# First cross attention of a four-layer kernel: a changed order of key projections, key parts and value casts

## The reference, cut to what matters

```python
x = x + _L0_xattn_ref(_layernorm(x), ctx, Wq, bq, Wkv, bkv, Wp, bp)

def _fq_sym(x, axis):            # fake quantisation to 127 steps
    s = max(max(abs(x), axis) / 127.0, 1e-08)
    return clip(round(x / s), -127, 127) * s

q = (x @ Wq + bq).reshape(1, 256, 16, 16)
kv = (cond @ Wkv + bkv).reshape(1, 4096, 2, 16, 16)
k, v = kv[:, :, 0], kv[:, :, 1]
q = _fq_sym(q * scale, axis=-1)  # one scale for a query and head
k = _fq_sym(k, axis=-1)          # one scale for a key and head
v = _fq_sym(v, axis=keys)        # one scale for a column, over all 4096 keys
attn = _fq_unsigned(softmax(q @ k.T), axis=-1)
return (attn @ v) @ Wp + bp
```

## Time and profile before

| | us |
|---|---|
| median of 3 runs | 1547.86 (1547.01 to 1548.96) |
| profiled execution, its own time | 1544.69 |
| its span, first to last instruction | 1542.9 |
| first stage in it, up to the last update of x | 0 to 332.4 |
| the loop over key pairs in it | about 8 to 142 |

### The profile page before, as it was taken

One profiled execution on the slowest core, in us unless ns is written; L12 is line 12 of the kernel. 1 busy time (PEld: TensorE's weight loads), 2 busy tenths in 40 slices (PEclk: granted clock), 3 DMA queues, 4 the chain that ended last, 5 costly groups with the idle time before them and its releaser, 6 DMA issues. The chain is left out here.

```text
span 1542.9 us, 23951 instructions
## 1 busy us (share of the span) xinstructions
PE 1380.5 (89%) x7964; PEld 978.2 (63%) x7964; DVE 1090.4 (71%) x2242; ACT 858.8 (56%) x2296; POOL 576.3 (37%) x643
## 2 busy tenths in 40 slices
PE   7867999966998789988789999999998989999979
PEld 5643444445866357767557778788877446666667
DVE  4688999925774665754568776675654779999963
ACT  2446999932124282435444645554554589999931
POOL 2236777730000002520536523532400047777710
PEclk9986999967999899997989999999999999999989
DMA  4000454554341404000200000000002343333110
GB/s 150 1 1 21 93 96 97 95 161 158 139 171 34 102 28 105 29 1 1 82 15 0 15 14 1 15 1 1 1 1 84 114 144 123 123 95 112 42 61 9
DMA packets 125073, 97.88 MB, mean 63 GB/s; under 512 B 84499, under 2 KB 100883, under 8 KB 124310
## 3 DMA queue, kind: packets, MB, share of 16 engines
q1 hardware_dynamic: 124950, 96.35, 21.6%
HBM read 79.28 MB, written 0.26 MB: 52 GB/s over the span
## 5 line engine op out<-in xcount | busy, mean ns | idle before, releaser
L601 ACT ACTIVATE x_v_full<-banks,x_neg_max,x_q_scale 128x1024 uint8<-128x1024 f32 x128 | 152.6, 1197 | 6.1 <-DMA x_v_full<-x_v_full 2.8
L708 DVE TENSOR_REDUCE x_row_max<-banks 128x1 f32<-128x512 f32 x248 | 151.6, 681 | 4.8 <-PE banks L381 4.8
L213 PE MATMUL banks<-a_w_ring,x_normed_T 128*128 128x512 f32 x320 | 146.4, 598 | 4.9 <-DVE a_r L3256 4.9
L538 POOL CAST x_v_full<-x_v_full 128x1024 f16<-128x1024 uint8 x128 | 131.5, 1044 | 50.4 <-DMA x_v_full<-x_v_full 46.2
L2735 DVE TENSOR_TENSOR ctx_tokens<-ctx_tokens,banks 128x512 f32<-128x512 f32 x128 | 87.8, 686 | 82.2 <-ACT x_weights_T L2621 60.3
L2453 PE MATMUL banks<-ctx_tokens,x_kT 128*128 128x512 f32 x272 | 140.0, 602 | 2.8 <-ACT ctx_tokens L2615 2.2
L2474 PEld LDWEIGHTS banks<-x_v,x_weights_T 128*128 128x128 f32 x896 | 113.0, 194 | 20.8 <-issue 17.5
L2474 PE MATMUL banks<-x_v,x_weights_T 128*128 128x129 f32 x896 | 118.1, 278 | 2.1 <-ACT x_weights_T L2631 2.1
L2569 POOL TENSOR_TENSOR ctx_tokens<-ctx_tokens 128x512 f32<-128x512 f32 (+1 forms) x48 | 65.9, 1373 | 141.4 <-DVE ctx_tokens L2715 141.4
L381 PE MATMUL banks<-x_kT_parts,x_qT_int 64*128 64x512 bf16 x512 | 109.8, 408 | 6.9 <-DVE x_row_max L708 4.1
L3146 POOL TENSOR_TENSOR a_rms<-a_rms,a_minus_half 128x4 f32<-128x4 f32 x64 | 64.9, 1014 | 115.7 <-ACT a_rms L3076 115.7
(11 more groups left out here) (533 smaller groups left out, 3278.6 us busy)
## 6 DMA issues: line engine op xcount, KB each, us to landing
a_w_ring<-in_L_attn_WB_T SPq DMA_DIRECT2D x16, 512.0 KB, 3.7
a_w_ring<-in_L_attn_WC_T SPq DMA_DIRECT2D x16, 512.0 KB, 5.5
f_w_gate_up<-in_L_ffn_gate_up SPq DMA_DIRECT2D x9, 736.0 KB, 4.3
f_w_down<-in_L_ffn_down SPq DMA_DIRECT2D x9, 512.0 KB, 5.2
ctx_tokens<-in_ctx SPq DMA_DIRECT2D x16, 256.0 KB, 6.2
x_wq<-in_L_xattn_Wq_T SPq DMA_DIRECT2D x8, 512.0 KB, 3.7
a_w_ring<-in_L_attn_Wth_T SPq DMA_DIRECT2D x8, 512.0 KB, 3.8
a_bias_ring<-in_L_attn_B_bias_perm SPq DMA_DIRECT2D x16, 256.0 KB, 4.9
```

The lines of the kernel that those rows point to most:

```text
L213: last = nc.tensor.matmul(out, lhsT, rhs, start=(i == 0), stop=(i == len(pairs) - 1))
L538: nc.gpsimd.tensor_copy(pf[:, q % WIDE], pt8[:, q % TURNED]).then_inc(s.unpacked, 1)
L601: nc.scalar.activation(eb[:, q % RING], k.ps[:, 2 + 2 * (q % 2):4 + 2 * (q % 2), :].rearrange("p a n -> p (a n)"), ACT.Exp, bias=nb[:, v % ...
L708: nc.vector.reduce_max(mx[:, u % 2, i:i + 1], k.bank(MBANK[m % 3]), AX.X).then_inc(s.max_taken, 1)
```

## The change

In the first stage:

- TensorE projects key pair j+1 in step j, ahead of the transposes of pair j-3 (in step 3 the query transposes come first). Pair 0 is projected in step 0 as before.
- ScalarE makes the middle part of pair j-1 ahead of the first part of pair j. The copy of the value scales (step 11) moves to the front of its step. In the last step with a key, 15, the copies of transposed pair 12 move ahead of the first part.
- The four casts of the values go from GpSimd (steps 13 to 16) to ScalarE (steps 12 to 15), in front of the first part.
- After its loop ScalarE evaluates one exponential of one element.
- VectorE combines the four maxima of the values two at a time in steps 4, 6 and 8, not in one reduction in step 8.

In `l0_ffn` the semaphore `first_pair` is replaced by the existing `w_loaded[11]`.

```diff
@@ TensorE
-                    if j < NP:
-                        project_keys(j)
+                    if j == 0:
+                        project_keys(0)
                     if j == 1:
                         project_queries()
                     if j == 3:
                         transpose_queries()
+                    if j + 1 < NP:
+                        project_keys(j + 1)
                     if j >= 3:
                         transpose_keys(j - 3)
@@ GpSimd
-                    if NP // 2 + 5 <= j < NP // 2 + 9:
-                        g = j - NP // 2 - 5
-                        pool.wait_ge(s.v_int_ready, g + 1)
-                        nc.gpsimd.tensor_copy(vq[:, VG * g:VG * (g + 1)], vi[:, g]).then_inc(s.v_ready, 1)
@@ ScalarE
+                    if j == NP // 2 + 3:
+                        act.wait_ge(s.vscale_in_psum, 1)
+                        nc.scalar.copy(vscale[:].rearrange("p r n -> p (r n)"), k.bank(7)).then_inc(s.vscale_ready, 1)
+                    if 1 <= j < NP + 1:
+                        m = j - 1
+                        act.wait_ge(s.rest_ready, m + 1)
+                        nc.scalar.copy(part(m, 1), kr[:, m % 2]).then_inc(s.mid_ready, 1)
+                    if j == NP - 1:
+                        take_keys(j - 3)
+                    if NP // 2 + 4 <= j < NP // 2 + 8:
+                        g = j - NP // 2 - 4
+                        act.wait_ge(s.v_int_ready, g + 1)
+                        nc.scalar.copy(vq[:, VG * g:VG * (g + 1)], vi[:, g]).then_inc(s.v_ready, 1)
                     if j < NP:
                         act.wait_ge(s.kf_ready, j + 1)
                         if j >= 3:
                             act.wait_ge(s.kT_in_psum, 2 * (j - 2))
                         nc.scalar.copy(part(j, 0), kf[:, j % 3]).then_inc(s.hi_ready, 1)
-                    if 1 <= j < NP + 1:
-                        m = j - 1
-                        act.wait_ge(s.rest_ready, m + 1)
-                        nc.scalar.copy(part(m, 1), kr[:, m % 2]).then_inc(s.mid_ready, 1)
...
-                    if j >= 3:
+                    if j >= 3 and j != NP - 1:
                         take_keys(j - 3)
-                    if j == NP // 2 + 3:
-                        act.wait_ge(s.vscale_in_psum, 1)
-                        nc.scalar.copy(vscale[:].rearrange("p r n -> p (r n)"), k.bank(7)).then_inc(s.vscale_ready, 1)
+                act.wait_ge(s.filled, 1)
+                nc.scalar.activation(warm[:], k.ones[0:1, 0:1], ACT.Exp)
@@ VectorE
                         link(nc.vector.tensor_reduce(vm[:, g], vf[:, VG * g:VG * (g + 1)].rearrange("p t d -> p d t"), AX.X, ALU.max, apply_absolute_value=True))
+                        if g == 1:
+                            link(nc.vector.tensor_tensor(vmax, vm[:, 0], vm[:, 1], ALU.max))
+                        if g == 2:
+                            link(nc.vector.tensor_tensor(vmax, vmax, vm[:, 2], ALU.max))
                     if j == NP // 2:
-                        nc.vector.tensor_reduce(vmax, vm[:].rearrange("p g d -> p d g"), AX.X, ALU.max).then_inc(s.vmax_ready, 1)
+                        nc.vector.tensor_tensor(vmax, vmax, vm[:, 3], ALU.max).then_inc(s.vmax_ready, 1)
```

More of the change, by code:

```diff
@@ L261, in l0_xattn @@
         attn = sb("attn", [P, B, D])
+        warm = sb("first_exp", [1, 1])
         vdiag = attn[:].rearrange("p r (c t) -> p r c t", c=DC)
@@ L844, in l0_ffn @@
         code = sb("fp4_code", [P, MLP_HALF], U16)
-        first_pair = ctx.enter_context(nc.semaphore("f0_first_pair"))
         def load(sp):
             sp.dma_start(wg[:], A["L0_ffn_gate_w_T"].rearrange("(c p) n -> p c n", p=P)).then_inc(k.w_loaded[2], 16)
-            sp.dma_start(wgu[:, 0], A["L0_ffn_gate_up"][0]).then_inc(first_pair, 16)
-            sp.dma_start(wd[:, 0], A["L0_ffn_down"][0]).then_inc(first_pair, 16)
+            sp.dma_start(wgu[:, 0], A["L0_ffn_gate_up"][0]).then_inc(k.w_loaded[11], 16)
+            sp.dma_start(wd[:, 0], A["L0_ffn_down"][0]).then_inc(k.w_loaded[11], 16)
         layernorm(k, load)
@@ L882, in gate_up @@
                     if n == 0:
-                        pe.wait_ge(first_pair, 32)
+                        pe.wait_ge(k.w_loaded[11], 32)
                     else:
```

## The result

| | before | after |
|---|---|---|
| median, its range, runs | 1547.43 (1546.38 to 1548.96), 4 | 1532.72 (1529.65 to 1536.07), 4 |
| profiled execution, its own time | 1544.69 | 1536.07 |
| its span | 1542.9 | 1534.3 |

The ratio is 0.9906, interval [0.989, 0.9922]: faster by 14.7 us, where 15.5 were forecast. The two profiled executions are only 8.6 us apart. That of before lies 1.7 us under the fastest of the four runs in the table, that of after is the slowest of its four, so the sizes of the steps are better read between marks inside the stage. The first key reaches VectorE at 17.52 us before and at 18.52 after, a difference that lies ahead of the change; I count from there.

The account below looks back on a forecast made before the run. Hand-overs between engines bound the second stretch, VectorE's row maxima (97% busy) the main loop. 4.0 + 1.4 + 1.1 + 1.5 + 5.7 - 1.9 + 2.0 + 1.1 + 0.6 = 15.5 us, giving 1532.4 us; range 1527.5 to 1539.5.

Parts of the forecast that it names:

- Query hole +4.0: First stretch: TensorE's 3.99 us idle time before the query transposes goes, as key pair 2 is projected earlier; gain 4.0 us.
- clock +1.4: Two sets of 16 query transposes, slowed by TensorE's lower clock level after the idle time, run faster; gain 1.4 us.
- one projection ahead +1.1: TensorE projects pair 8 in front of the transposes of pair 4, which no longer delay it; gain 1.1 us.
- rival 2: TensorE's idle time before the query transposes stays, the margin being 0.4 us; 5.4 us less gain, 1537.8 us; chance 0.08.
- +1.5: VectorE's 1.89 us reduction over the values becomes a two-input maximum of 0.42 us; gain 1.5 us.
- +5.7: Second stretch: VectorE's waits shrink, 2.7 us for projections and 3.0 for the value scales; gain 5.7 us.
- Interference +2.0: VectorE's scale instructions and key products are slowed less once value casts leave GpSimd; gain 2.0 us, 2.5 still allowed.
- late last cast -1.9: Last step with a key: ScalarE's value cast, priced at 1.8 us, no longer hides behind VectorE; loss 1.9 us.
- Rival 1: VectorE and GpSimd get in each other's way in every step; 6.7 us less gain, 1539.1 us; chance 0.13.
- Tail +1.1: Last first part to the first head's last row maximum: two ScalarE copies move ahead, GpSimd's subtraction partly shows; gain 1.1 us.
- Table +0.6: Exponential table load, 1.28 us before the first exponential, moves beside the preceding work; VectorE's 0.60 us wait goes; gain 0.6 us.
- Rival 4: Main loop: TensorE stays at its lower clock; 24 slow quarter heads cost 15.5 us, all 128 end near 1614; chance 0.03.

Follow-up runs that it names:

- again: Unchanged kernels run once more for a second profile: the changed kernel 1532.72 us (ratio 0.9904), the kernel before 1547.79 us (ratio 0.9999).
- the pairs: Changed kernel with one DMA transpose for two quarters (64 in place of 128): 1520.2 us, ratio 0.9817; the same edit in the kernel before: 1534.63 us.

## Why the prediction was right

Counted from the first key, with the two "again" profiles where they bear on it:

- **Query hole +4.0, clock +1.4, one projection ahead +1.1.** The query transposes come 4.16 us earlier, key 8 6.4 earlier (62.04 to 55.61), where 6.5 were forecast. The margin of 0.4 us held, so rival 2 is out; the kernel without TensorE's order shows the hole at its old 3.99.
- **Up to the last key**, the terms named so far with +1.5, +5.7 and +2.0 make 15.7; measured 15.6. The reduction of the values was shown by itself at 1.5, TensorE's order by itself at 9.0 for its forecast 9.2 (4.0, 1.4, 1.1 and 2.7). That 15.7 met 15.6 is in part luck. VectorE's scale instructions and key products, over keys 8 to 15 and above their undisturbed 0.18 and 0.69 us, lose 4.7 us before and 3.5 after: interference gave 1.2 where 2.0 were forecast. The waits gave the difference back: what is left of the second stretch's 9.15 us behind that 1.2 and the 1.5 of the reduction is 6.5, for a forecast of 5.7. And of the 5.7 the split between the two orders did not hold: TensorE's alone takes 2.5 from the second stretch, the rest without it 8.9, where 6.5 were forecast (1.5, 2.0 and 3.0).
- **Interference +2.0** and **late last cast -1.9**: putting the casts back shows the move itself at 2.1 and 1.9. The +2.0 was a net figure, though, and the net is the 1.2 above: of the 4.7 us 3.5 are left, where 2.5 had been allowed, since a fuller VectorE meets GpSimd oftener (with the casts on GpSimd it is 5.6). The cast took 1.90 us, where a straight line through two shorter copies gave 1.8. Rival 1 (every step hit) fell, though GpSimd's subtraction was hit in half of them: four of the last eight took 2.0 to 2.5 us, each beside a value product. The next product of a key was hit only now and then (1.58 at 48.13 us). The Trainium skill (GPSIMD Engine Reference, Key points) names VectorE instructions with two SBUF inputs as those that contend with GpSimd. By that rule the trace agrees: the value product reads two SBUF tiles, and the subtraction beside it went from 1.16 to 2.49 us. The prediction drew from the rule that the last key product would be hit; it took 2.30 us before, beside a cast on GpSimd, and 0.69 after, when GpSimd was idle (116.44 us).
- **Tail +1.1**: mis-sized, 0.5. The last key to the last maximum took 1.4 us longer (10.21 to 11.59), where 0.8 was forecast from +1.1 and -1.9; with the casts on GpSimd it took 9.72, 0.5 less than before. The kernel with the middle part behind has nearly the same tail (11.42). The likely reason, as the rows have it: the subtraction of the last pair itself (1.15 us at 120.12) still has to pass before the middle part can start, and with the late cast the two copies were no longer what it stood behind. That last clause is a reading of the time line and was not tried by itself.
- **Table +0.6**: 0.3 to 0.4. From the last maximum to the first exponential 2.53 us became 0.82; 1.28 of these 1.7 are the load, and the other 0.4 comes from no edit that was taken out singly (the gap is 0.82 or 1.25 in variants with the early load, 2.10 or 2.53 in kernels without it). From the last maximum to quarter 20 the gain is 0.35 us (29.74 to 29.38), and without the one-element exponential it goes. The prediction was right to discount a gain in front of a busy loop, but named the wrong engine for it: where the head start is lost, ScalarE waits for TensorE at its lower clock. Rival 4 had said that with a denser start nothing is lost; the denser start lost the head start of 1.4 us.
- **"In the main loop VectorE sets the pace"**, and at the head of the prediction "VectorE is 97% busy [...] so that stretch moves as a block". The block did move as one, from quarter 20 to quarter 60 within about 0.1 us, so the sum took no harm; the reading was wrong all the same. SyncE's issues set the length of the loop, as the pairs show, and VectorE 97% busy could lose 57 us of work and leave the time where it was.
- The Trainium skill (ScalarE: Activation LUTs, What ACT_TABLE_LOAD costs) would have a further 1.38 us for a drain. No trace here shows it: the exponential starts 1.29 to 1.30 us after the load begins, with and without the early one.

At quarter 20 the change has given 14.6 us: 15.6, less 1.4 for the tail, plus 0.35 for the table. The medians say 14.7 and 15.3. The forecast of 15.5 is 0.9 above the 14.6, of which the tail makes 0.6 and the table 0.3. Rival 3 (1528.0) and rival 5 (1547) lie outside of what was measured. Rival 4's loss of 15 us or more fell with the windows: 0.53 in the 18 us after the first exponential as before, then 1.00.

The difference between the profiled spans would have misled anyone who took it for the gain. In the first profile of the kernel before, the last issue to the second stage took 9.9 us (9.6 without the one-element exponential), in all others with single transposes 12.3 to 13.1, also in the second profile of before (12.8). In the first profile of before the last landings had been lucky: in the changed kernel's second one, with 12.8 us, a 16 KB load of instructions went out on its own DMA queue at 310.1 us and the last cast waited 2.0 us for its transpose. About a dozen such loads fall into the main loop, and the long issues and late landings (up to 4.9 us, median 2.4) lie beside them. That they cause them is read from their times alone; no run took them away.

## What to carry to other kernels

A chain that loses time at hand-overs can be costed from its rows: each idle gap in front of an instruction, with what released it, gave its term within a microsecond, and the sum of the terms better than each by itself. Which edit earns a term is another question: two orders could each remove the same waits. Look for a gain at a mark well inside the stretch that follows, too: of 1.7 us won in front of the main loop 0.35 were left twenty quarters later. But a share of 97% is no proof that an engine sets the pace: ask what would happen if it were lighter, and look at the queues that only issue, whose time is in no busy share. Here 128 issues of 1.31 us each filled the loop from end to end, and one issue for two pieces gave almost as much as the whole change.

Two moves can cancel almost exactly (casts off GpSimd: 2.1 gained in the loop, 1.9 lost in the tail), and a change can then carry parts that are worth nothing. Only taking them out singly shows it.

## What the runs showed of the hardware

- A DMA transpose of 128x512 two-byte elements holds SyncE's queue for 1.22 us and one of twice the size for 1.23 us; it lands 2.4 and 2.7 us after its issue (medians). Until these runs I had taken the issue for something that rides along. That the cost goes by the issue and not by the bytes is shown for these two sizes alone.
- The stretch from the first exponential to the second stage took 188.3 and 191.8 us in two executions of the kernel before, 194.0 and 192.2 in two of the changed one, while the 111 or 127 us in front of it repeated within 0.1 us. Of the 4.2 us between the two profiled spans of before 3.5 are made there, of the 4.6 us between those of after 1.8.
- A scale instruction on VectorE of 128x32 elements, 0.18 us undisturbed, had a mean of 0.46 us beside GpSimd's work in the changed kernel and 0.57 before.
